# Local attention in two layers on one core: the floor under the sums of squares as Relu and a bias of the logarithm on ScalarE, in place of a clamp on VectorE

## What is computed

```python
def l2norm(t):
    return t / jnp.clip(jnp.linalg.norm(t, axis=-1, keepdims=True), 1e-12)

def _layer(x, wqkv, qs, ksc, wo, lg, lb, w1, b1, w2, b2):
    h = shift_token(x)
    q, k, v = jnp.split(h @ wqkv, 3, axis=-1)
    ...
    q = l2norm(q) * qs
    k = l2norm(k) * ksc
    q, k = rotary_xpos(q, k)
    o = local_attention(q, k, v)
    x = x + o @ wo
    ...
```

## Time and profile before

| what | value |
|---|---|
| runs | 1243.13, 1244.14, 1346.53 us; median 1244.14 us |
| the profiled execution | 1243.1 us, of which 1241.3 us is the span from its first to its last instruction |
| mean granted TensorE clock | 0.977 of full speed |
| steps of the two local stages | from about 175 to 460 us and from about 545 to 830 us |

### The profile page before, as it was taken

How to read it: one execution, slowest core, us unless ns; L and a number is a source line. 1 busy time by engine, 2 the same in 40 slices (tenths; PEclk the granted TensorE clock), 3 DMA queues, 4 the chain that set the end, 5 groups by cost and what they waited for, 6 DMA issues and landing times.

```text
span 1241.3 us, 33606 instructions
## 1 busy us (share of the span) xinstructions
PE 1102.4 (89%) x11412; PEld 923.9 (74%) x11412; DVE 1059.5 (85%) x2403; ACT 901.3 (73%) x2552; POOL 731.8 (59%) x1088
## 2 busy tenths in 40 slices
PE   6899968888898879977989888889979998899996
PEld 4777746777777769966777777768967776699996
DVE  4899968999999967878999999958879998399988
ACT  4888847878787775547787878775568888676762
POOL 4799827666665654435656566554378996344431
PEclk9999989999999999999999999999999999799999
DMA  6000001010101012101112210011100000000000
GB/s 194 17 2 2 7 11 26 22 27 21 27 22 27 17 30 57 35 21 27 25 23 44 73 27 22 21 25 27 30 4 2 2 2 2 1 14 14 14 14 18
DMA packets 62409, 30.80 MB, mean 25 GB/s; under 512 B 46197, under 2 KB 56481, under 8 KB 62242
## 3 DMA queue, kind: packets, MB, share of 16 engines
q1 hardware_dynamic: 59474, 27.15, 9.2%
q10 hardware_dynamic: 2768, 1.51, 0.4%
HBM read 9.77 MB, written 2.10 MB: 10 GB/s over the span
## 4 chain that ended last, share of the span: by engine, by line
PE 39%; DVE 30%; issue 17%; ACT 10%; POOL 3%; DVEq 1%; DMA 0%; ACTq 0%; POOLq 0%
PE m_ps_y L1508 6%; DVE a_stat L1169 6%; DVE a_stat L1161 6%; PE a_ps_a L962 4%; DVE a_rot L1125 3%; DVE x_e L691 3%; PE f_ps_y L1295 3%; DVE a_rot L1123 3%; PE f_ps_g L1306 3%; PE a_ps_qk L919 2%; PE f_ps_a L1313 2%; ACT a_e L1102 2%; PE m_ps_h L1495 2%; ACT x_e L652 2%; PE m_ps_h L1497 2%
## 5 line engine op out<-in xcount | busy, mean ns | idle before, releaser
L1102 ACT ACTIVATE a_e<-a_ps_s,a_stat 128x128 f32<-128x128 f32 x512 | 227.4, 481 | 4.3 <-DVE a_stat L1173 4.2
L1235 POOL TENSOR_TENSOR a_rot<-a_rot 128x512 f32<-128x512 f32 x64 | 82.7, 1292 | 201.3 <-DVE a_rot L1125 201.3
L1229 POOL TENSOR_TENSOR a_e<-a_e,a_stat 128x1024 f32<-128x1024 f32 x64 | 121.6, 1900 | 5.8 <-DVE a_stat L1150 5.8
L1102 ACT ACTIVATION_READ_ACCUMULATOR a_e<-a_ps_s,a_stat 128x1 f32 x512 | 117.1, 229 | 0.0
L1040 PE MATMUL a_ps_t<-c,a_e 128*128 128x128 f32 x512 | 70.0, 281 | 49.7 <-DVE a_qT L1180 49.4
L1040 PEld LDWEIGHTS a_ps_t<-c,a_e 128*128 128x128 f32 x512 | 56.4, 144 | 56.8 <-issue 54.3
L1342 ACT ACTIVATE f_gl<-f_ps_g,vec 128x128 f32<-128x128 f32 (+1 forms) x192 | 55.9, 361 | 58.0 <-PE f_ps_g L1306 57.1
L1069 ACT ACTIVATE a_stat<-a_stat 128x16 f32<-128x16 f32 x64 | 13.8, 216 | 110.2 <-DVE a_stat L1163 110.0
L1223 POOL TENSOR_TENSOR a_rot<-a_rot 128x512 f32<-128x512 f32 x64 | 81.9, 1279 | 18.2 <-DVE a_rot L1125 18.2
L740 DVE TENSOR_REDUCE x_stat<-x_ps_s 128x16 f32<-128x1024 f32 x64 | 77.1, 1205 | 11.9 <-PE x_ps_s L546 11.9
L1123 DVE TENSOR_TENSOR a_rot<-a_ps_qk,a_rtab 128x512 f32<-128x512 f32 x128 | 86.9, 679 | 0.0
(11 more groups left out here) (204 smaller groups left out, 3700.6 us busy)
## 6 DMA issues: line engine op xcount, KB each, us to landing
a_vx<-a_vt SPq DMA_DIRECT2D x64, 128.0 KB, 2.3
a_h<-y SPq DMA_DIRECT2D x64, 32.0 KB
f_h<-y SPq DMA_DIRECT2D x64, 32.0 KB
out_dram<-x SPq DMA_DIRECT2D x32, 64.0 KB, 1.5
a_h<-y SPq DMA_DIRECT2D x64, 31.8 KB
f_h<-y SPq DMA_DIRECT2D x64, 31.8 KB
w<-in_L_ffn_w_dram SPq DMA_DIRECT2D x2, 768.0 KB, 5.6
x<-in_x_dram SPq DMA_DIRECT2D x1, 768.0 KB, 5.4
```

What stands on the lines that cost most here:

```text
L1102: act.activation(self.e[n % 2][:, P * i:P * i + P], ps_s[:, P * i:P * i + P], ACT.Exp, bias=stat[:, 24 + i:25 + i], scale=stat[:, root:roo ...
L1229: p.tensor_tensor(e3, e3, self.stat[n % UNROLL][:, 16:24].unsqueeze(2).broadcast_to([P, 8, P]), ALU.mult)\
L1235: p.tensor_tensor(r, r, self.rot2[:, INNER:], ALU.add).then_inc(self.s_n, 1)
```

## The change

The clamp on VectorE goes. Its floor is done on ScalarE: a Relu of the sum minus 1e-24, in place, ahead of the logarithm, and 1e-24 times 2^16 as the logarithm's bias, so that `Ln(2^16 * relu(x - 1e-24) + 2^16 * 1e-24)` is the logarithm of `2^16 * max(x, 1e-24)`. The upper bound of 2^48 goes without a replacement. Both constants stand in two columns of `small`, set once by GpSimd at the start with two more `memset` of 128x1. In a round ScalarE now does the Relu where the logarithm stood, the logarithm where the exponential stood, and the exponential one place later, after the copy of the transposed keys. `s_ss` counts one per tile and `s_rt` three, and all waits on them follow.

```diff
-NORM_CAP = 2.0 ** 48
+NORM_FLOOR = 1e-24
...
+        self.floor_down, self.floor_up = small[:, 16:17], small[:, 17:18]
...
-            for t, value in ((g.neg_half, -0.5), (g.one, 1.0)):
+            for t, value in ((g.neg_half, -0.5), (g.one, 1.0), (g.floor_down, -NORM_FLOOR), (g.floor_up, NORM_FLOOR * 2.0 ** ROOT_SHIFT)):
                 p.memset(t, value).then_inc(self.s_clear, 1)
-            p.wait_ge(self.s_clear, 2)
+            p.wait_ge(self.s_clear, 4)
...
-            act.wait_ge(self.s_ss, 2 * k + 2)
-            act.activation(t[:, 32:48], t[:, 32:48], ACT.Ln, scale=2.0 ** ROOT_SHIFT).then_inc(self.s_rt, 1)
+            act.wait_ge(self.s_ss, k + 1)
+            act.activation(t[:, 32:48], t[:, 32:48], ACT.Relu, bias=g.floor_down).then_inc(self.s_rt, 1)
         n = s - 1
         if 0 <= n < T:
             k = T * l + n
             act.wait_ge(self.s_qk, 2 * k + 1)
-            after(act, self.s_ss, 2 * k - 1)
+            after(act, self.s_ss, k)
             act.activation(self.sq[:, 0:INNER], ps_qk[:, 0:INNER], ACT.Square).then_inc(self.s_sq, 1)
         n = s - 2
         if 0 <= n < T:
             k, t = T * l + n, self.stat[n % UNROLL]
-            act.wait_ge(self.s_rt, 2 * k + 1)
-            act.activation(t[:, 48:64], t[:, 32:48], ACT.Exp, scale=-0.5).then_inc(self.s_rt, 1)
+            act.wait_ge(self.s_rt, 3 * k + 1)
+            act.activation(t[:, 32:48], t[:, 32:48], ACT.Ln, bias=g.floor_up, scale=2.0 ** ROOT_SHIFT).then_inc(self.s_rt, 1)
...
+        n = s - 2
+        if 0 <= n < T:
+            k, t = T * l + n, self.stat[n % UNROLL]
+            act.wait_ge(self.s_rt, 3 * k + 2)
+            act.activation(t[:, 48:64], t[:, 32:48], ACT.Exp, scale=-0.5).then_inc(self.s_rt, 1)
...
             v.wait_ge(self.s_sq, 2 * k + 2)
-            after(v, self.s_rt, 2 * (k - 4) + 2)
-            norms = self.stat[n % UNROLL][:, 32:48]
-            v.reduce_sum(norms, self.sq[:, :].rearrange("p (h d) -> p h d", d=LD), axis=AX_X).then_inc(self.s_ss, 1)
-            v.wait_ge(self.s_ss, 2 * k + 1)
-            v.tensor_scalar(norms, norms, 1e-24, NORM_CAP, ALU.max, ALU.min).then_inc(self.s_ss, 1)
+            after(v, self.s_rt, 3 * (k - 4) + 3)
+            v.reduce_sum(self.stat[n % UNROLL][:, 32:48], self.sq[:, :].rearrange("p (h d) -> p h d", d=LD), axis=AX_X)\
+                .then_inc(self.s_ss, 1)
```

More of the change, by code:

```diff
@@ L302, in totals @@
                 (self.s_mc, 32), (self.s_g, 32), (self.s_val1, 16), (self.s_key1, 32), (self.s_bk, 80), (self.s_bq, 64), (self.s_rest, 32),
-                (self.s_clear, 2), (self.s_tanh, 1), (self.s_c16, 1), (self.s_k, 4), (self.s_ks, 4), (self.s_kl, 4), (self.s_md, 4),
+                (self.s_clear, 4), (self.s_tanh, 1), (self.s_c16, 1), (self.s_k, 4), (self.s_ks, 4), (self.s_kl, 4), (self.s_md, 4),
                 (self.s_mk, 2), (self.s_km0, 2), (self.s_mr, 1), (self.s_vp, 4), (self.s_ve, 4), (self.s_vq, 4), (self.s_v1, 4)]
@@ L1171, in vector @@
             v.wait_ge(self.s_mx, 3 * k + 1)
-            v.wait_ge(self.s_rt, 2 * k + 2)
+            v.wait_ge(self.s_rt, 3 * k + 3)
             v.tensor_tensor(stat[:, 24:32].rearrange("p (e r) -> p e r", e=2), stat[:, 0:8].rearrange("p (e r) -> p e r", e=2),
@@ L1239, in gpsimd @@
             p.wait_ge(self.s_n, 2 * k + 1)
-            p.wait_ge(self.s_rt, 2 * k + 2)
+            p.wait_ge(self.s_rt, 3 * k + 3)
             r = self.rot[n % 2][:, INNER:].rearrange("p (h d) -> p h d", d=LD)
```

## The result

The changed kernel takes 1175.82 us in the median of 4 runs (1174.67 to 1176.44). The kernel before took 1245.62 us in the median of its 4 runs by then. One of these four, at 1346.53 us, was a slow one, and the ratio leaves it out. The ratio is 0.9445, with a 95% interval of 0.9423 to 0.9466: 5.6% faster. The forecast was 1188 with a range of 1177 to 1209. The profiled execution took 1174.67 us, 68.4 less than the 1243.1 of before, where the sum had 55.5.

What follows compares the result with a forecast made beforehand. The prediction took a ring through VectorE and TensorE, with the clamp stalled by GpSimd, as the bound; 54 rounds times 0.99 us plus 2 us, 55.5 off 1243.1, gave 1188 us, range 1177 to 1209.

Steps and rivals of the forecast that it cites:

- the sum: Whole kernel: 54 steady rounds times 0.99 us, plus 2 us from the other ten clamps, 55.5 us gained.
- What bounds the kernel, and the stall: VectorE's queue: the clamp takes 1.46 us, stalled until GpSimd's multiplication into a_e ends, in a ring through VectorE and TensorE.
- The rings: Steady round without the clamp: ScalarE with TensorE 7.62 us, VectorE with TensorE 7.58, GpSimd with VectorE 7.47, TensorE alone 7.74.
- The ring of 7.47 through GpSimd: From line 1235 through GpSimd's a_e and VectorE's line 1180 back to 1235: 5.51 plus 1.96 us.
- The round: Steady round in the local stages: from 8.74 to 7.75 us, a gain of 0.99, with ends of 7.58 and 8.1.
- TensorE alone: TensorE's busy time per steady round, 7.74 us, taken as the longest ring; 7.6 to 7.8 once it waits no more.
- The rest of the sum: Clamps at the starts of the stages: the other ten hold 5.5 us, of which 2 were taken as gained.
- What comes: ScalarE's added work: Relu and biased logarithm 320 ns each, mostly in waits; moved exponential about 0.1 us in a ring.
- Rival 1: VectorE's line 1173 stalls on GpSimd instead, 0.4 us on the path: round 7.99 us, time 1201; chance 0.13.
- Rival 2: ScalarE becomes the bound, the copy of the keys waiting for the logarithm: round 8.0 us, time 1202; chance 0.12.
- Rivals 3 and 4: Added table loads on ScalarE, about 1316 us, chance 0.02; a hidden wait, round above 8.3, 1220 to 1244, chance 0.05.
- its own lowest case: Low end of the forecast time: a round of 7.58 us with all of the ten clamps' 5.5 us gained, 1175.

Runs made afterwards that it cites:

- e9: Kernel before, with GpSimd's multiplication into a_e on 4 of its 8 blocks, clamp left alone: round 7.89 us, time 1195.24 us.
- e2: Changed kernel plus an idle clamp in the old place on VectorE's queue, which nobody waits for: round 8.74 us, time 1241.35 us.
- e1: Kernel before, with the floor on VectorE written as a maximum over pairs, upper bound left out: round 7.57 us, time 1176.94 us.
- e10: Changed kernel plus an idle 128x16 copy on ScalarE right ahead of the eight exponentials: round 7.73 us, time 1181.27 us.
- e3: Changed kernel without the Relu, logarithm and exponential in their old places, floor left to the logarithm's bias: round 7.57 us, time 1176.65 us.
- e4: Changed kernel with the exponential put back ahead of the copy of the transposed keys: round 7.58 us, time 1176.16 us.
- e5: Changed kernel without half the products of weights and values and half the heads' k-half rotation: round 7.63 us, time 1177.68 us.
- e12: Changed kernel with 4 of the 8 transposes of the exponentials left out: round 7.63 us, time 1178.50 us.
- e8: e3 with the rotation of the k half on 4 of 8 heads: round 7.51 us, time 1167.14 us.
- e11: Changed kernel plus an idle 128x16 copy on ScalarE right behind the Relu: round 7.62 us, time 1180.32 us.

## Why the prediction was right or wrong

**What bounds the kernel, and the stall: right.** The clamp was stalled until GpSimd's multiplication ended (e9), in VectorE's queue and not by its result (e2), and because of its form (e1). Of the 68.4 us gained, 62.9 lie between the first and the last reduction of line 1161 in the two local stages.

**The rings: right.** Predicted were 7.62 for ScalarE's, 7.58 for VectorE's with TensorE. Measured: 7.62 in the changed kernel, moved by what is put into ScalarE's ring or taken out of it (e10, e3, e4) and not by cuts on the other two engines (e5, e12); 7.57 for VectorE's (e3 against e8). The ring of 7.47 through GpSimd was never the longest, and no run tests its length.

**The round: wrong, and this is the larger of the two steps that failed.** The prediction had "TensorE alone: 7.74 us busy per round ... so 7.6 to 7.8 once it waits no more" and took 7.75 for the round. TensorE alone needs at most 7.51 (e8), and it is busy 7.62 us of 7.62 in the changed kernel with the same instructions. Busy time is no lower bound, because it counts a matmul to its end and the next one can begin before that. Before, the transposes of the exponentials had ended, at 307.23, when the k half began at 307.40 behind its wait:

```profile
306.17 1.06 PE L1040 MATMUL a_ps_t<-c,a_e 128*128 128x128 f32 x8 [0.79 <-DVE a_qT L1180]
```

In the changed kernel they end at 306.61 + 1.09 = 307.70, and the k half has begun at 307.55. The longest ring built from starts was 7.62, and that was the round. I had also let the four rings get in each other's way, up to 8.1. In the changed kernel they do not. Between the sixth and the last reduction of a layer lie 26 rounds, and the two layers gained 29.6 and 29.3 us there, 58.9, where 52 times 0.99 are 51.5. That is 7.4 of the 12.9 us missing. This alone does not carry the time out of the range: with 7.62 for the round the sum would have given 1243.1 - 54 x 1.12 - 2 = 1180.6. The next term did the rest.

**The rest of the sum, the other step: 4.0 priced, 9.5 found.** For the first five rounds of each layer and the round after the last reduction I had 2 + 2 x 0.99. The first five gained 4.1 together. Behind layer 0's last reduction it is 1.4 less, and behind layer 1's 3.7, up to the end of the kernel, which holds stages that the change does not touch; 0.4 more lie ahead of the first reduction. Most of the 3.7 is TensorE's clock. The same instructions at the start of the experts' stage, from VectorE's instruction at 1045.39 to that at 1099.97, take 54.6 us before, and from 979.42 to 1031.57 they take 52.2 after. The first row is a piece of that stretch before, and the other two are the whole of it, before and after:

```profile
1060.00:1067.00 7.00, 5.84 (x18) 4.97 (x19) 4.97 (x30) 3.76 (x6) 2.95 (x8) 0.50 0.00 0
...
1045.40:1100.00 54.60, 47.72 (x302) 39.80 (x300) 32.96 (x122) 37.80 (x70) 19.71 (x52) 0.87 0.02 5
...
979.40:1031.60 52.20, 44.68 (x302) 37.17 (x301) 32.90 (x122) 37.74 (x70) 19.67 (x52) 0.93 0.02 5
```

By the clock records of the traces TensorE had the lower of its two levels (1.2 of 2.4 GHz) for 13.7 us of this stretch before and for 6.8 after. All 14 profiles of this case have the stretch, and its length follows that number: 52.2 us where it is 6.8 (two profiles), 53.0 to 53.8 where it is 10.2 (eight), 54.6 where it is 13.7 (four). So 2.4 of the 3.7 us go with the clock and not with the work of the stages. Whether the change brings the better clock or the single execution does, no run tells: the four runs of the changed kernel have mean clocks of 0.980 to 0.982, those of e3, with a round as short, 0.973 to 0.978. In the two starts of five rounds the kernel before spent 13.7 us at the lower level and the changed kernel 10.2, so some of the 4.1 us may be of the same kind; how much, no run separates.

The spread of the experiments fits that too. The changed kernel, e5, e11 and e12 all have rounds of 7.62 to 7.63, and profiled times of 1174.7, 1177.7, 1180.3 and 1178.5. Their first five rounds, both layers together, took 69.5, 69.9, 74.5 and 73.0 us, with 10.2, 12.9, 23.9 and 17.1 us at the lower level. What e5 has beyond the changed kernel lies mostly behind the local stages, where it has 33.7 us at the lower level against 21.3.

**What comes: right in size.** 308 and 299 ns against 320. The Relu lay in cover (e11, and e4 against e3). The moved exponential is in the ring and costs 0.04 to 0.05 per round against 0.1, since VectorE's ring is next at 7.57.

**Rival 1, the stall moves on to the product of maximum and inverse root: the mechanism is there, the price is not.** The median is 196 ns against 167, where I expected 300 to 500. The row before is:

```profile
L1173 DVE TENSOR_TENSOR a_stat<-a_stat x64: 166/167/682, 191.9 to 827.9; 128x8 f32<-128x8 f32 x64
```

In the round above GpSimd ends at 305.37 and line 1177 at 305.40, ahead of the copies that the transposes release at 305.52. At its longest, in the starting rounds, it took 919 ns. The instruction of 0.61 us in the earlier trace rows is of the same kind. That is the rule of the Trainium skill, "SBUF — State Buffer", "Who interferes with whom", on two inputs in SBUF, and the trace agrees. For the clamp and the reductions the same section says that a `tensor_scalar` can lock and a `tensor_reduce` never does, and e1 and e2 agree, with 0.19 us beside 1.57.

**Rival 2, ScalarE as the bound, was half right.** Its ring is the longest, but at 7.62 and not at 8.0; the copy of the keys did not have to wait for the logarithm, which ended at 305.44, 0.08 ahead. **Rivals 3 and 4** did not come: the changed kernel's count of table loads is that of before, and no hidden wait turned up.

**The range** was cut from the ends of the round (7.58 to 8.1) with its low end at 1177 instead of at the 1175 that its own lowest case gave. The 1175 would have held the measured 1175.82, though that case had all of the ten clamps' 5.5 us for its reason, and not the clock. The clock had no term in the sum: the 13 runs of the kernel before beside e1 to e4 go from 1241.06 us at a mean granted clock of 0.979 to 1249.25 at 0.968.

## What to carry to other kernels

A small VectorE operation that ends each time when a GpSimd instruction ends is waiting and not working. Another form of the same operation at the same place can be the cure: here a reduction over pairs did as well as moving the clamp to ScalarE. After a stall goes, add up the rings from starts to starts, and expect the longest one to be the round, as it was here; an engine's busy time per round is no lower bound on it, since it holds overlaps, and an engine can be busy in every microsecond and still follow another's pace. The same small copy on ScalarE was free where that engine waited and cost 0.10 us per round where the ring passed, so look at the place in the queue before you look at the operation. Where two kernels have the same round and different times, compare the granted clock over the same instructions: here 6.8 us more at the lower level went with 2.4 us of time.

## What had not been expected of the hardware

Two sets of matmuls on different halves of the array's columns run side by side so fully that leaving one set out changes neither the length of a matmul group (0.28 us against 0.29) nor the distance to the next (0.11 to 0.12 us). And nearly all steady rounds of a kernel agree within 0.02 us, while the starts of the stages vary by up to 5 us in sum between kernels with the same steady round, with the time that TensorE spends at its lower clock.
